# Projections, read-outs and MLP sums of the small-head attention stages moved to other slots

## What is computed

```python
def _L0(x, latents, attention_mask, ...):          # 16 heads of 16, 512 keys: ctx and x
    h = jnp.concatenate([x, latents], axis=1)
    ...
    attn = jnp.where(full_mask[:, None, None, :], attn, -jnp.inf)
    ...
    out = gelu(rmsnorm(attn_out) @ mlp_w1 + mlp_b1) @ mlp_w2 + mlp_b2
def _L1(...):                                      # 16 heads of 128, two cross attentions, MLP
    x = x + cross_attention(ln(x), ctx, ...)       # twice
    return x + gelu(ln(x) @ w_fc1) @ w_fc2
def _L2(...):                                      # 16 heads of 16, self, then cross, then MLP
    scores = scores * mask - 10000.0 * (1.0 - mask)
    probs = jax.nn.softmax(scores, axis=-1)
    ...
def _L3(...):                                      # 32 query heads of 8 on 8 key heads
    scores = scores + encoder_attention_mask
    attn = jax.nn.softmax(scores, axis=-1)
    ...
    return layernorm(out @ Wo + bo + hidden_state) * gamma + beta
```

## Time and profile before

| | |
|---|---|
| median of 3 runs | 1596.28 us (1591.95 to 1596.41) |
| the profiled execution | 1595.42 us |
| its span in the trace | 1593.6 us |
| PE, PEld busy | 1489.5 us, 1147.4 us |
| DVE, ACT busy | 934.5 us, 907.3 us |
| POOL busy | 144.6 us |

### The profile page before, as it was taken

The page is one execution under the profiler, slowest core; times in us unless marked ns, Lnnn a source line. Parts: engine busy times, 40 slices in busy tenths (PEclk is TensorE's granted clock), DMA queues, the critical chain, the costliest instruction groups (busy, mean ns, idle before and its releaser), DMA issues. The chain is left out here.

```text
span 1593.6 us, 28683 instructions
## 1 busy us (share of the span) xinstructions
PE 1489.5 (93%) x9824; PEld 1147.4 (72%) x9824; DVE 934.5 (59%) x3314; ACT 907.3 (57%) x2807; POOL 144.6 (9%) x163
## 2 busy tenths in 40 slices
PE   7999999999999999999999999997897888988886
PEld 5666687888787787778787878785665657866554
DVE  4777624545454455545554555318989992278886
ACT  5788824444443443444444434337888884398885
POOL 2000010000000001000000000101222311012200
PEclk9999999999999999999999999998999999999998
DMA  7000103010100101001010000001001000000000
GB/s 285 2 2 2 62 1 119 1 47 15 47 15 1 61 1 61 1 1 61 1 61 1 1 0 1 1 1 54 1 2 41 9 8 7 1 4 6 22 4 12
DMA packets 10879, 40.66 MB, mean 26 GB/s; under 512 B 2416, under 2 KB 2672, under 8 KB 8688
## 3 DMA queue, kind: packets, MB, share of 16 engines
q1 hardware_dynamic: 10736, 38.82, 6.9%
HBM read 37.77 MB, written 1.05 MB: 24 GB/s over the span
## 5 line engine op out<-in xcount | busy, mean ns | idle before, releaser
L943 ACT ACTIVATE probs<-probs,negmax 128x256 f32<-128x256 f32 (+1 forms) x640 | 347.2, 548 | 77.8 <-DVE negmax L1186 77.4
L1017 ACT ACTIVATE pT<-bank 128x512 f32<-128x512 f32 x128 | 76.4, 597 | 388.0 <-PE bank L761 388.0
L558 PEld LDWEIGHTS bank<-ident,probs 128*128 128x128 f32 x1536 | 178.6, 147 | 95.0 <-issue 44.2
L558 PE MATMUL bank<-ident,probs 128*128 128x128 f32 x1536 | 233.8, 290 | 10.0 <-DVE pT L1194 6.3
L1309 DVE TENSOR_REDUCE stats<-bank 128x1 f32<-128x257 f32 x256 | 108.4, 425 | 212.3 <-PE bank L753 211.3
L1186 DVE CUSTOM_DVE_ANT_0 probs<-bank,mask_a 128x256 f32<-128x256 f32 (+1 forms) x384 | 178.4, 508 | 50.4 <-PE bank L545 42.1
L951 ACT ACTIVATE pT<-bank 128x512 f32<-128x512 f32 x288 | 168.8, 587 | 25.6 <-PE bank L558 25.3
L545 PE MATMUL bank<-kT,q_res 32*128 32x256 f32 (+1 forms) x1280 | 112.6, 458 | 36.6 <-DVE negmax L1186 29.3
L772 PE MATMUL bank<-pT,probs 128*128 128x256 f32 x512 | 132.7, 381 | 2.7 <-ACT pT L1017 2.7
L753 PE MATMUL bank<-kT,pT 128*128 128x257 f32 x512 | 132.7, 382 | 0.6 <-ACT pT L1000 0.6
L943 ACT ACTIVATION_READ_ACCUMULATOR probs<-probs,negmax 128x1 f32 x640 | 124.8, 195 | 0.0
(11 more groups left out here) (110 smaller groups left out, 2490.6 us busy)
## 6 DMA issues: line engine op xcount, KB each, us to landing
w_m<-in_w SPq DMA_DIRECT2D x6, 1024.0 KB, 6.9
g_qkv<-in_g SPq DMA_DIRECT2D x4, 1536.0 KB, 6.9
q_res<-in_g SPq DMA_DIRECT2D x4, 1536.0 KB, 6.7
w_qkv<-in_w SPq DMA_DIRECT2D x3, 768.0 KB, 4.3
g_bv<-in_gbv SPq DMA_DIRECT2D x8, 256.0 KB, 7.0
g_o<-in_go SPq DMA_DIRECT2D x4, 512.0 KB, 3.4
q_res<-in_go SPq DMA_DIRECT2D x4, 512.0 KB, 3.5
rows<-in_rows SPq DMA_DIRECT2D x1, 1664.0 KB, 14.3
```

The source lines that it names most:

```text
L558: last = nc.tensor.transpose(out[:, n * P:(n + 1) * P], probs[:, u % PROBS, q * T + t * P:q * T + (t + 1) * P], ident[:, :])
L943: last = nc.scalar.activation(s, s, ACT.Exp, bias=negmax[:, u % PROBS, k:k + 1], scale=-1.0, accum_out=sums[:, tile % 2, q, j * c.res + r: ...
```

## The change

It moves instructions and changes no arithmetic. One activation of 128x2 is new.

- **One slot for a projection.** Both halves of a projection, and both of y, are now issued in one slot. Stage 2: q 5, k 8, y 11, v 14, turn of rows 3 of the part after. Stage 3: q 3, k 7, v 15, y 11. Stage 0: k0 3, y 11, q 15, turn of rows 19, k1 23, v0 27, v1 31.
- **Read-outs.** `after` in stage 2 is three slots earlier in VectorE's own count instead of one: `outputs` in 11 and 3, `add_outputs` in 8, `norm_rows` in 10, `values` in 11. In stages 0 and 3 it stays the end of the quad. ScalarE's `keys` now stand before the exponential of their slot.
- **MLP sums.** VectorE adds the last MLP sums behind the maxima of unit 1 (`mlp_sums`); for stage 2 their statistics follow in slot 6 and `norm_rows` in slot 8, and GpSimd's `power` moves into its slot 6.
- **Stage 0's start.** The first scores are issued ahead of v1's projection; `values("v1", 0)` is VectorE's in slot 2; ScalarE does an exponential of `half` before it waits for the weights.
- **Mask products.** Those of the first quad of stage 2 are behind maxima 0 (one) and 1 (two).

```diff
     def y_slot(self, p):
-        return self.tile_slot(2 * p + 1) + 4
+        return self.tile_slot(2 * p + 1) + 5
     def norm_slot(self, p):
-        return self.y_slot(p) + 6
+        return self.y_slot(p) + (6 if self.kinds == "mult" else 8)
...
+    def y_taken(self, p):
+        return self.after(self.y_slot(p))
     def after(self, slot):
-        return slot - 1 if self.kinds == "mult" else slot | (QUAD - 1)
+        return slot - 3 if self.kinds == "mult" else slot | (QUAD - 1)
...
-        at = [3, 6, 13] if self.kinds == "mult" else [2, 6, 14] if len(self.loads()) == 3 else [2, 6, 14, 22, 26]
+        at = [5, 8, 14] if self.kinds == "mult" else [3, 7, 15] if self.host else [15, 3, 23, 27, 31]
...
-                    for n in range(2):
-                        for what, p in c.projected(s - n) if s >= n else []:
-                            project(what, p, n)
+                    for what, p in c.projected(s):
+                        project(what, p, 0)
+                        project(what, p, 1)
...
-            for s in range(c.count + 2):
+            for what in ("q", "k0", "k1", "v0"):
+                project(what, 0, 0)
+                project(what, 0, 1)
+            slot(0)
+            project("v1", 0, 0)
+            project("v1", 0, 1)
+            for s in range(1, c.count + 2):
                 slot(s)
...
+            act.wait_ge(sem("s_half"), 1)
+            nc.scalar.activation(negmax[:, 0, :], half[:, :], ACT.Exp)
...
+                    if c.host and slot == 1:
+                        mlp_sums(1 if c.name == "2" else 2, B - 1)
+                    if c.host and slot == 6 and NORMS[c.host][0] != "raw":
+                        row_stats(c.host, B - 1, x_rows)
+                    if c.host and slot == 8:
+                        norm_rows(c.host, B - 1, x_rows)
...
-                        if c.after(c.y_slot(p) + 1) == slot:
+                        if c.y_taken(p) == slot:
                             add_outputs(p)
...
-                    for s in range(max(slot - 4, 0), slot + 1):
+                    for s in range(max(slot - 3, 0), slot + 4):
                         for what, p in c.projected(s):
-                            if c.after(s + 1) == slot and what == "q" and not c.spread(what, p):
+                            if c.after(s) == slot and what == "q" and not c.spread(what, p):
                                 queries(p)
```

More of the change, by code:

```diff
@@ L590, in reciprocals, with outputs @@
                     last.then_inc(sem("a_rt"), 1)
[L592 to L595, removed]
+                def outputs(p):
+                    free(c.use("y", p))
+                    pe.wait_ge(sem("a_oout"), st.at("a_oout", 0, 2 * p + 2))
                     wo = w_o[c.parts[p].w]
[L597 to L601, removed]
+                    for q in range(QT):
+                        for i in range(KT):
+                            last = mm(bank[7][:, q * D:(q + 1) * D], oT[:, p % 2, i, q * P:(q + 1) * P], wo[:, i, :],
+                                      start=(i == 0), stop=(i == KT - 1))
+                    last.then_inc(sem("a_proj"), 1)
                 def slot(s):
@@ L959, in attention @@
                         turned(slot - c.copy_lag)
+                    ahead = c.turn_lag - c.copy_lag
+                    for what, p in c.projected(slot + ahead - 1) if slot + ahead >= 1 else []:
+                        if c.by_scalar(what, p):
+                            keys(what, p)
                     if slot < c.count:
                         exps(slot)
-                    ahead = slot - 1 + c.turn_lag - c.copy_lag
-                    for p in [p for x in range(ahead if slot else 0, ahead + 1) for p in c.normed(x)]:
+                    for p in c.normed(slot + ahead):
                         name, b = (c.host, B - 1) if p < 0 else (c.parts[p].norm, c.parts[p].b)
@@ L966, in attention @@
                             take_rows(name, b, bank[7])
-                    for what, p in c.projected(ahead) if ahead >= 0 else []:
-                        if c.by_scalar(what, p):
-                            keys(what, p)
             def mlp(n, gelu, before, own, keys=None):
@@ L1111, in take_rows, with mlp_sums @@
                 last.then_inc(sem("l_hv"), 1)
+            def mlp_sums(n, b):
+                st = S[f"m{n}"]
+                added(dve, f"m{n}", b)
+                dve.wait_ge(sem("m_y"), st.at("m_y", b, 1))
+                for q in range(QT):
+                    xq = x_rows[:, b * QT + q, :]
+                    last = v.tensor_tensor(xq, bank[4 + q][:, 0:D], xq, ALU.add)
+                last.then_inc(sem("m_out"), 1)
+                dve.wait_ge(sem("m_out"), st.at("m_out", b, 1))
             def projections_of(c):
@@ L1235, in attention @@
                     dve.wait_ge(sem("s_const"), 64)
-                    for what in c.loads():
-                        if what[0] == "v":
-                            values(what, 0)
+                    values("v0", 0)
                 if c.kinds == "mult":
@@ L1281, in mlp @@
                         values("v0", 0)
-                    added(dve, f"m{n}", b)
-                    dve.wait_ge(sem("m_y"), st.at("m_y", b, 1))
-                    for q in range(QT):
-                        xq = x_rows[:, b * QT + q, :]
-                        last = v.tensor_tensor(xq, bank[4 + q][:, 0:D], xq, ALU.add)
-                    last.then_inc(sem("m_out"), 1)
-                    if NORMS[own][0] != "raw":
-                        dve.wait_ge(sem("m_out"), st.at("m_out", b, 1))
-                        row_stats(own, b, x_rows)
+                    if b < B - 1 or not queries:
+                        mlp_sums(n, b)
+                        if NORMS[own][0] != "raw":
+                            row_stats(own, b, x_rows)
             def wide(j, before, own):
@@ L1496, in after2 @@
                 c = SMALL[1]
+                if slot == 6:
+                    power("l21", B - 1)
                 if slot == 12:
```

37 lines of the change are left out of this document (16 added, 21 removed).

## The result

The changed kernel takes 1610.4 us (median of 4 runs, 1607.2 to 1612.5), the kernel before 1596.3 in the same comparison: a ratio of 1.0093, 95% interval 1.0069 to 1.0117. It is slower by 14 us. The profiled execution took 1609.84 us with a span of 1608.1, 14.5 more than the span before.

A forecast was written before the change was run, and what follows sets the result against it. It took TensorE to bound stage 0, nearly VectorE stage 2 (a ring through three engines), no full engine stage 3. Terms -1.0 + 6.2 + 4.2 - 3.5 - 1.2 - 1.0 = +3.7 on 1595.42 gave 1599 us, range 1579 to 1608.

The forecast's parts named there:

- stage 0: Stage 0: shorter waits on TensorE and an earlier first maximum, second scores 0.2 us later; -1.2 us (-7.7 to +1.9).
- stage 2, start: Start of stage 2: second scores about 4 us sooner, first part's maximum of slot 12 at 1103; -1.0 us (-4 to +1).
- stage 2, ring and clock, seven parts: Stage 2: six parts at 31.5 us, +6.2, the last 0; TensorE's half clock in seven parts, +4.2.
- stage 2, end: End of stage 2: `outputs` before the last maximum of slot 12, last times_v near 8 us behind it; -3.5 us.
- stage 3: Start of stage 3: two maxima fill VectorE's 2.38 us wait for the last MLP sums; -1.0 us (-1.9 to 0).
- The old ring: Stage 2, add, `values`, turn of rows, ScalarE, y, add: 30.86 us; it opens and TensorE's 3.11 us wait goes.
- The new ring through the add in slot 8: Stage 2, maximum of slot 12, ScalarE's work, y, add, VectorE's work to the next maximum: 31.5 us a part.
- ScalarE: 18.5 us: Stage 2, ScalarE without a pause from the end of slot 12's maximum through the k read-out: 18.5 us.
- The last part: Last part of stage 2, 29.35 us before, with no q, k or v to project: charged 0.
- the clock alone pays: Rival: stage 2 waits as before, but every part like the one of 29.98 us; 1586 us, chance 0.14.
- the slower rival: TensorE's clock falls in both gaps of a stage 2 part, behind y and before slot 0; 1603 to 1609 us, chance 0.24.
- VectorE full: Rival: y done before slot 8, so stage 2 parts cost 28.4 us; 1576 to 1583 us, chance 0.16.

The follow-up runs named there:

- the early read-outs alone: Kernel before with only `after` at slot - 3 in stage 2 and the loop over `s` widened to match: 1614.1 us, ratio 1.013.
- the filler run: Changed kernel with 16 extra 128x128 transposes on TensorE behind y in slot 11 of every stage 2 part: 1607.0 us, ratio 1.0085.
- the last run: Changed kernel with `after` at slot in stage 2, `values` at slot - 1, and mask products of slots 8 and 9 done twice: 1578.3 us, ratio 0.9907.
- the fastest one: Changed kernel with `after` at slot in stage 2 and `values` left at slot - 1: 1577.4 us, ratio 0.9893.

## Why the prediction was wrong, point by point

The forecast was 1599, no difference that can be measured; slower by over 0.3% had a chance of 0.32. 1610.4 lies 2.4 us beyond the range. The end of maximum 12 is the mark that the sum used: first part 1104.01 before and 1104.38 after, last part 1316.09 and 1333.96.

| term | predicted | measured |
|---|---|---|
| stage 0 | -1.2 | +0.3 |
| stage 2, start | -1.0 | 0 |
| stage 2, ring and clock, seven parts | +6.2 + 4.2 = +10.4 | +17.5 |
| stage 2, end | -3.5 | -2.8 |
| stage 3 | -1.0 | -0.6 |
| sum | +3.7 | +14.4 |

- **The old ring opens: right.** The waits for `v_two` ahead of the turn of rows are gone. The description of the change put the turn in slot 3 and the prediction moved it "back by three slots"; `y_slot` + 6 is slot 1 of the part after, one slot later, as the order of instructions also shows. Nothing in the sum came from the other two slots.
- **The new ring through the add in slot 8: right as a mechanism.** The added work on ScalarE and behind the add shows, the same work ahead of the add doesn't.
- **The size of the ring: the step that failed.** The step "ScalarE: 18.5 us" counted ScalarE without a pause from the maximum to k. It is 19.8: exponential 4 waits 0.59 us for its maximum, a copy 0.2, exponential 12 starts 0.12 behind its maximum, k takes 0.83 instead of 0.71, and 0.2 is spread over the rest. The prediction itself named a ScalarE that isn't continuous as what would make it wrong altogether. The 0.59 comes from the wait for the reciprocals in slot 3, which the prediction allowed up to 1.8 us and called hidden by the later wait at the add. It is 2.46 us, and VectorE's maxima behind it are what ScalarE needs: with `outputs` late that wait is 0.18, exponential 4 doesn't wait, and from exponential 12 to the next add it takes 21.07 us instead of 21.81. Why the reciprocals come so late is open. Q (1.9 us) and times_v stand ahead of them, but with q in halves in slots 3 and 4 (the early read-outs alone) they start 12.0 us behind exponential 12 instead of 12.3. "Y: 2.0" measured 2.2. VectorE's 11.0 us from the add to maximum 12 was right: 10.9 in the filler run; at half clock it is 11.4. Without the slow clock the ring is 32.8 instead of 31.5, beyond the bound of 32.5 that stood in the text.
- **The last part and the ends: wrong.** The six parts of 182.83 us already hold the last one of 29.35, so the sum charged it 31.5 and then, once more, nothing. The reason given for the nothing, that the ring loses 2.2 us where nothing is projected, fails: it took 32.3 us, only 1.0 less than the parts before it, since its ring has the same add in slot 8 and the same wait for the maximum. What was truly left at nothing are the stretches from the first maximum 12 to the first add and from the last add to the last maximum 12: 31.0 us together instead of 29.3.
- **The clock: right in the mean, partly by luck.** 0.6 a part was charged, half of a price of 1.2 behind y; 0.5 was measured, as 0.5 to 0.6 behind y in three parts of six and 0 to 0.9 behind the other gap in three. The two gaps were forecast at 2.4 and 2.1 us and measured 2.63 and 0.8 to 1.7. That the clock alone pays (a rival) and that it takes both gaps of a part (the slower rival, whose time of 1603 to 1609 came out nearly) are both not what happened: with the filler the kernel is still 13 us slower than before. The gap ahead of the turn of rows went, and two others came in its place: the mean granted clock of the six parts is 0.93, 0.92 before. The rule of the Trainium skill that was weighed (TensorE: Matmul & The Clock Gate, Part 1: half rate unless activity releases it) agrees with the filler run, where more work gave more clock; a gain for this change doesn't follow from it.
- **Stage 2's start: a small miss in each of two terms.** The second scores come 3.6 us sooner (1081.87 against 1085.49), near the 4 forecast. But `outputs` and `values` ahead of the maximum, with waits of 1.07 and 0.85 us, took all of that and not three quarters. Alone the seam gives 3.1, 3.5 if counted from the stage's own first scores.
- **Stage 0.** The k0 wait of 0.98 us for `v_two` and second scores 0.8 us later (0.2 had been allowed) cancel what the steady parts gain. Some of the 0.8 is the execution: with the old start unchanged they came at 20.96, 21.35 and 21.48 us in three kernels, and at 21.77 here.
- **Stage 3** can't be read from one execution: with its code unchanged, in the run of the early read-outs alone, it took 201.9 us from its first `v_four` to the end of the span, and 205.4 in the kernel before. So the -0.6 of the table shows nothing.
- **VectorE full (1576 to 1583)** was worked out for a case in which y comes before slot 8. It is what the change becomes with later read-outs (1579.8 and 1577.4), though the last run shows that VectorE itself isn't what limits it then.

- **A slip in the rivals.** The -5.7 for seams and stages 0 and 3 in two of them is -6.7 by the prediction's own terms; both times would be 1 us lower, and no chance hangs on it.

The sum was 10.7 us short. 7.1 of them are stage 2 between its first and last maximum 12: six rounds of 32.6 us instead of 31.5 without the slow clock are 6.6, the ends that were left at nothing 1.8, and the clock took 1.2 less than was charged. The rest are seams and stages 0 and 3, each of which gained 0.4 to 1.5 us less than forecast.

## What to carry to other kernels

- In a program of fixed orders, a read-out that is moved ahead of its producer makes the reading engine wait, and everything queued behind it waits too. Let it stand as late as its buffer's next user allows; here, from slot - 1 to slot - 3, each slot earlier cost about 2 us a part, and the delay from slot - 1 to slot still gained 0.3. Where later becomes too late, no run here shows.
- A ring through several engines is only found by going round it with every wait counted, the small ones too: a wait that "is hidden by the next one" still delays what other engines need from the instructions between the two.
- Whether an engine is on the ring is told by adding the same work ahead of its wait and behind it. Busy shares didn't tell: VectorE was 85% busy in the changed kernel, where its work behind the add set the time, and 94% busy in the fastest one, where 1 us more of it cost nothing.

## What the runs showed of the hardware

- The granted clock is not decided by the length of one wait. In the changed kernel a times_v behind a wait of 2.63 us took 1.93 us, granted clock 0.50, and 1.07 us in three other parts, behind the same wait at the same place; with mask products added on VectorE behind the add, the times_v behind a wait of 2.62 us at the same place took 1.07 us and the part kept 1.00:

```profile
1231.82 1.07 PE L584 MATMUL bank<-pT,v_two 128*32 128x256 f32 x16 [2.62 <-ACT pT L955]
```

- A TensorE instruction of the same form takes 1.07 or 1.93 us by the clock alone, yet the whole effect on a part of 33 us was 0.5 us: of VectorE's two read-outs behind it `outputs` didn't wait at all, and `values`, which reads a v that was done some 1.6 us later than in the filler run, waited 0.37 us.
